# A residual stack of four attention and feed-forward pairs: the first attention in units of 512 tokens, and all attentions with token-major values

## The reference

```python
x = x + xattn0(layernorm(x), ctx, mask, Wq, Wkv, Wo)             # a0: 2 heads of 64, full mask
x = x + ffn0(layernorm(x), w_gate, w_up, w_down)                 # f0: quantised gated FFN
x = x + xattn1(layernorm(x), ctx, ...)                           # a1: 16 heads of 8, biases
x = x + ffn1(layernorm(x), expert_sel, keys, values, ...)        # f1: 16 small experts, top 4
x = x + xattn2(layernorm(x), ctx, mask, ...)                     # a2: 16 heads of 8, rotary, key mask
x = x + ffn2(layernorm(x), ...)                                  # f2: product keys, gated FFN
x = x + xattn3(layernorm(x), ctx, ...)                           # a3: 16 heads of 8, biases
x = x + ffn3(layernorm(x), ...)                                  # f3: 8 experts, top 2, shared ones

def attention(x, context):                                       # the core of a0 to a3
    q, k, v = split_heads(x @ Wq + bq), split_heads(context @ Wk + bk), split_heads(context @ Wv + bv)
    scores = einsum('bhqd,bhkd->bhqk', q, k) * scale             # masked with -inf in a0 and a2
    out = einsum('bhqk,bhkd->bhqd', softmax(scores), v)
    return merge_heads(out) @ Wo + bo
```

## Time and profile before

| | |
|---|---|
| median of the runs | 1361.57 us |
| profiled execution, its own time | 1361.15 us |
| its span, first to last instruction | 1359.4 us |
| mean granted TensorE clock | 0.901 |
| busy: TensorE, VectorE, ScalarE, GpSimd | 1061.9, 988.6, 624.9, 339.9 us |
| a0, first matmul to f0's layer norm | 16.93 to 141.43 us |
| f0 to the first step of a1's layer norm | to 307.32 us |
| steady batches of a1 | 6.07 us apart |
| steady batches of a2 | 6.92 us apart |

### The profile page before, as it was taken

The page is one execution under the profiler, slowest core; times in us unless marked ns, Lnnn a source line. Parts: engine busy times, 40 slices in busy tenths (PEclk is TensorE's granted clock), DMA queues, the critical chain, the costliest instruction groups (busy, mean ns, idle before and its releaser), DMA issues.

```text
span 1359.4 us, 21524 instructions
## 1 busy us (share of the span) xinstructions
PE 1061.9 (78%) x7235; PEld 685.3 (50%) x7235; DVE 988.6 (73%) x2359; ACT 624.9 (46%) x972; POOL 339.9 (25%) x350
## 2 busy tenths in 40 slices
PE   2766780067996998799669888888878969999998
PEld 1544430064553775454326666566654536566665
DVE  4687669977786566577689788788567875666665
ACT  2211356735763334665266555555447633333332
POOL 0121000001220001444198767677201210000000
PEclk9888796578998999899859888888999998999999
DMA  7000000001000000000000000000000000000000
GB/s 264 0 1 0 0 0 0 0 1 58 2 2 1 1 1 0 1 2 1 1 1 1 2 1 0 1 0 0 1 1 2 1 1 1 16 8 8 8 8 16
DMA packets 7797, 14.12 MB, mean 10 GB/s; under 512 B 800, under 2 KB 5024, under 8 KB 7328
## 3 DMA queue, kind: packets, MB, share of 16 engines
q1 hardware_dynamic: 7712, 13.05, 2.9%
HBM read 10.95 MB, written 2.10 MB: 10 GB/s over the span
## 4 chain that ended last, share of the span: by engine, by line
PE 44%; DVE 37%; issue 11%; ACT 6%; DVEq 1%; SPq 1%; DMA 0%; POOL 0%; ACTq 0%
DVE big L1127 6%; DVE big L1122 6%; PE psum L1997 4%; PE psum L919 4%; PE psum L2000 4%; PE psum L2011 4%; PE psum L1692 3%; DVE big L1903 2%; PE psum L1484 2%; DVE tmp L1868 2%; PE psum L1437 2%; PE psum L1446 2%; PE psum L247 2%; ACT psum L1760 2%; DVE amax L1247 2%
## 5 line engine op out<-in xcount | busy, mean ns | idle before, releaser
L1122 DVE TENSOR_REDUCE big<-psum 128x16 f32<-128x1024 f32 x96 | 114.4, 1221 | 74.7 <-PE psum L873 38.7
L1817 POOL TENSOR_TENSOR big<-big 128x512 f32<-128x512 f32 x128 | 134.7, 1087 | 20.7 <-ACT big L1740 20.7
L2047 ACT ACTIVATE big<-psum 128x512 f32<-128x512 f32 x80 | 47.9, 598 | 143.3 <-PE psum L1997 143.2
L1760 ACT ACTIVATE psum<-big,tmp 128x512 f32<-128x512 f32 x128 | 85.0, 687 | 42.3 <-DVE big L1903 38.4
L1903 DVE SCALAR_TENSOR_TENSOR big<-big,tmp,psum 128x512 f32<-128x512 f32 x128 | 90.4, 743 | 4.7 <-ACT psum L1760 1.8
L790 POOL TENSOR_TENSOR big<-big,w_const 128x256 f32<-128x256 f32 x48 | 34.8, 726 | 233.3 <-PE psum L919 219.3
L2100 DVE TENSOR_TENSOR big<-big,psum 128x512 f32<-128x512 f32 x80 | 54.4, 687 | 53.1 <-PE psum L2000 52.5
L1827 POOL TENSOR_TENSOR big<-big 128x1024 f32<-128x1024 f32 x32 | 75.4, 2367 | 70.4 <-DVE big L1903 70.4
L1127 DVE RECIPROCAL big<-psum 128x256 f32<-128x256 f32 x48 | 84.0, 1749 | 11.8 <-PE psum L919 11.8
L2011 PEld LDWEIGHTS psum<-tmp,big 128*128 128x128 f32 x512 | 66.7, 191 | 40.1 <-issue 36.4
L1028 ACT ACTIVATE big<-psum 128x1024 f32<-128x1024 f32 x64 | 62.0, 1021 | 51.5 <-PE psum L903 51.5
(11 more groups left out here) (252 smaller groups left out, 2484.2 us busy)
## 6 DMA issues: line engine op xcount, KB each, us to landing
out<-X SPq DMA_DIRECT2D x8, 256.0 KB, 2.3
tmp<-in_pack_f SPq DMA_DIRECT2D x1, 1924.0 KB, 7.5
w_f<-in_pack_f SPq DMA_DIRECT2D x1, 1280.0 KB, 12.3
ctxd<-in_ctxd SPq DMA_DIRECT2D x1, 1024.0 KB, 6.4
tmp<-in_pack_once SPq DMA_DIRECT2D x1, 960.0 KB, 8.6
w_a<-in_pack_a SPq DMA_DIRECT2D x3, 256.0 KB, 12.0
w_f<-in_pack_f SPq DMA_DIRECT2D x1, 576.0 KB, 9.5
w_const<-in_pack_const SPq DMA_DIRECT2D x1, 560.0 KB, 3.9
```

What stands on the lines that cost most here:

```text
L1122: dve.tensor_reduce(nm, psum[:, 1 + 2 * t:3 + 2 * t, :].rearrange("p c (r l k) -> p (c r) l k", r=2, k=SK), AX.X, ALU.max, negate=True).th ...
L1760: act.activation(bank(EX_BANK + h % 2), ssum[t][:, h * 512:(h + 1) * 512], ACT.Exp, bias=shift2[:, t * NH2 + h:t * NH2 + h + 1]).then_inc( ...
L1817: ins = pool.tensor_tensor(ssum[t][:, h * 512:(h + 1) * 512].rearrange("p (i j) -> p i j", i=ROWS2), st[:, 0, h, 0:ROWS2].unsqueeze(2).to_ ...
```

## The change

**a0** is a new function set (`att0_pe`, `att0_act`, `att0_dve`, `att0_pool`), unrolled over eight units of 512 tokens. Keys and values of all batches are built once, by ScalarE with a mask as its scale. The negated maxima are no longer transposed: GpSimd adds them to the mask (`less_max`), and the matmul with the identity in ST that brought the mask now brings both. PV has the probabilities as its stationary operand and, as moving one, two heads' values of 64 columns, each with a column of ones behind it (130 columns). Its output is token-major, with one sum per head and token, so that the reciprocal has 8 elements; `TO` transposes the result for `O`. From group 3 on GpSimd normalises. The three steps on f0's quantised weights stand in units 3 to 5, with the rounding made by an int16 output.

**a1 to a3** get the same PV: probabilities stationary (128x128), two heads' values of 8 columns and a ones column each moving (18). The sums are 32 per token, `norm` writes `ow`, `TO` transposes it, `take_out` on ScalarE evicts, and `O` follows one iteration later. In the iteration PV's second half, MX and Q now stand ahead of O, NM, TO. GpSimd no longer builds values.

**The layer norm** has 10 VectorE steps with fewer waits, and takes 1/sqrt as exp(-0.5 ln) in two ScalarE steps from one table set; in a0 it is done in two parts (12 and 20 tiles). **The context** is loaded once (512 KB); a value block is two matmuls with 64 output partitions each. X is loaded in two parts, and the first 12 tiles stand ahead of everything.

```diff
@@ loads
-            sp.dma_start(pack_sb["const"][:, :], dram["pack_const"]).then_inc(S("ld_const"), 16)
-            sp.dma_start(X[:, :, :], dram["x"].rearrange("(t p) d -> p t d", p=P)).then_inc(S("ld_x"), 16)
+            sp.dma_start(X[:, 0:LN0, :], x_in[:, 0:LN0, :]).then_inc(S("ld_x"), 16)
+            sp.dma_start(pack_sb["const"][:, :], dram["pack_const"]).then_inc(S("ld_const"), 16)
             sp.dma_start(pack_sb["a0"][:, :], dram["pack_a0"]).then_inc(S("ld_a0"), 16)
-            sp.dma_start(ctxd[:, :, :, :].rearrange("p b a k -> p (b a k)"), dram["ctxd"]).then_inc(S("ld_ctx"), 16)
+            sp.dma_start(ctx_sb[:, :, :].rearrange("p b k -> p (b k)"), dram["ctx"]).then_inc(S("ld_ctx"), 16)
             sp.dma_start(mask_u8[:, :], dram["mask"]).then_inc(S("ld_mask"), 16)
+            sp.dma_start(X[:, LN0:N_TILES, :], x_in[:, LN0:N_TILES, :]).then_inc(S("ld_x"), 16)
@@ heads_pe
-            def PV(b, which):
+            def PV(b, t):
...
-                for e in range(2):
-                    for r in range(4):
-                        w = W["vmask8"][:, 32 * e:32 * e + 32] if which else \
-                            L.vw[b % 2][:, 64 * r + 32 * e:64 * r + 32 * e + 32]
-                        ins = pe.matmul(bank(6)[32 * r:32 * r + 32, 256 * which:256 * which + 256], w,
-                                        L.pt[b % 2][:, (2 * r + e) * 256:(2 * r + e + 1) * 256],
-                                        start=(e == 0), stop=(e == 1))
+                for c in range(8):
+                    ins = pe.matmul(bank(6)[:, 144 * t + 18 * c:144 * t + 18 * c + 18],
+                                    L.pt[b % 2][:, c * 256 + t * P:c * 256 + (t + 1) * P],
+                                    L.vw[:, b, c].rearrange("p e n -> p (e n)"), start=True, stop=True)
+            def TO(b):
+                pe.wait_ge(hs("ow"), hat(s, "ow") + b + 1)
+                pe.wait_ge(hs("nmT"), hat(s, "nmT") + min(b + 4, B))
...
+                for t in range(2):
+                    ins = pe.transpose(bank(5)[:, 256 + t * P:256 + (t + 1) * P], L.ow[b % 2][:, t * P:(t + 1) * P], ident)
@@ heads_act
                 exp(b, 1)
                 if b + 1 < B:
                     takeN(b + 1)
+                if b >= 2:
+                    take_out(b - 2)
                 norm_half(b)
@@ heads_dve
-                dve.reciprocal(L.rz, bank(6)[:, 256:512]).then_inc(hs("rz"), 1)
+                both = bank(6)[:, 0:288].rearrange("p (h n) -> p h n", n=9)
+                dve.reciprocal(L.rz[b % 2], both[:, :, 8]).then_inc(hs("rz"), 1)
...
-                dve.tensor_tensor(L.oT[b % 2], bank(6)[:, 0:256], L.rz, ALU.mult).then_inc(hs("oT"), 1)
+                dve.tensor_tensor(L.ow[b % 2].rearrange("p (h n) -> p h n", n=8), both[:, :, 0:8],
+                                  L.rz[b % 2].unsqueeze(2).to_broadcast([P, 32, 8]), ALU.mult).then_inc(hs("ow"), 1)
@@ att0_pe, the loop
+            for i in range(N_GROUPS):
+                ST(i)
+                if i + 2 < N_GROUPS:
+                    Q(i + 2)
+                if i + 1 < N_GROUPS:
+                    MX(i + 1)
+                PV(i)
+                if i:
+                    O(i - 1)
+                if i + 3 < N_GROUPS:
+                    T(i + 3)
+                TO(i)
@@ att0_dve, ahead of and in the loop
+            mx(1)
+            dve.wait_ge(S("bn0"), N_TILES)
+            dve.sem_inc(sem(s, "stats"), 1)
+            ln_finish_dve(dve, s, 1)
+            for i in range(N_GROUPS):
+                if i and i + 1 < N_GROUPS:
+                    mx(i + 1)
+                over(i)
+                if i:
+                    add(i - 1)
+                    tail_stats(dve, s, i - 1, False)
+                if 3 <= i < 6:
+                    f0_weights_dve(dve, i - 3)
@@ att0_pool
+            for g in range(N_GROUPS):
+                less_max(g)
+                if g + 3 < N_GROUPS:
+                    norm(g + 3)
@@ ln_finish_act
-            act.activation(lnw[:, 5, :], lnw[:, 4, :], ACT.Sqrt).then_inc(sem(s, "std"), 1)
+            act.activation(lnw[:, 5, lo:hi], lnw[:, 4, lo:hi], ACT.Ln).then_inc(S("all_lnv"), 1)
+            act.wait_ge(S("all_lnv"), SUB.index(s) + k + (s != "a0") + 1)
+            act.activation(lnw[:, 6, lo:hi], lnw[:, 5, lo:hi], ACT.Exp, scale=-0.5).then_inc(sem(s, "std"), 1)
```

More of the change, by code:

```diff
@@ L722, in build, with ctx_keys, context_values @@
-        HSUB = ("a1", "a2", "a3")
-        PER = dict(k_ps=1, v_ps=4, k=8, kb=2, ka=2, v=4, zero=2, mask=0, kv=B, q_ps=B, qe=0, qT=B, q16=B, mx_ps=2 * B,
-                   mx=2 * B, nm_ps=B, nmT=B, st_ps=B, pt=2 * B, pv=B, rz=B, oT=B, o_ps=B, r=0, prep=0)
-        PRIMED = dict(mx=2, nmT=1, pt=2, pv=4, oT=1, o_ps=2)
+        ctx_sb = sb("ctx", [P, B, SK])
+        def ctx_keys(b, n):
+            return ctx_sb[:, b:b + n, :]
+        def context_values(pe, out, b, w):
+            for a in range(2):
+                ins = pe.matmul(out[64 * a:64 * a + 64, :], ctx_sb[:, b, :], w, start=True, stop=True)
+            return ins
@@ L746, in __init__ @@
                 self.kbd16 = a.take(B * 512, BF16).rearrange("p (b u n) -> p b u n", b=B, u=2)
-                self.V2 = a.take(B * P).rearrange("p (b n) -> p b n", b=B)
-                self.vw = [a.take(256) for _ in range(2)]
+                self.vw = a.take(B * 144).rearrange("p (b c e n) -> p b c e n", b=B, c=8, e=2)
                 self.pt = [a.take(2048) for _ in range(2)]
@@ L754, in __init__ @@
                 self.oT = [a.take(256) for _ in range(2)]
-                self.rz = a.take(256)
+                self.ow = [a.take(256) for _ in range(2)]
+                self.rz = [a.take(32) for _ in range(2)]
                 if rope:
@@ L807, in heads_pool @@
                 rotate(1)
-                weights(0)
                 rotate(2)
-                weights(1)
                 rotate(3)
@@ L840, in V @@
                 if i:
[L841 removed]
+                    pe.wait_ge(hs("v"), hat(s, "v") + 2 * i)
                 for m in range(4):
[L843 to L844 removed]
+                    ins = context_values(pe, bank(5)[:, m * P:(m + 1) * P], 4 * i + m, W[s + "_wv"])
                 ins.then_inc(hs("v_ps"), 1)
@@ L960, in heads_pe @@
                 turn_ahead(b)
-            for b in range(B + 2):
+            for b in range(B + 4):
                 if b < B:
@@ L1073, in heads_act @@
                 act.wait_ge(hs("mask"), hat(s, "mask") + 2)
-            for b in range(B):
+            for b in range(B + 2):
+                if b >= B:
+                    take_out(b - 2)
+                    continue
                 exp(b, 0)
@@ new lines, in build @@
+        m16 = a0m.take(N_TILES * P, BF16).rearrange("p (t n) -> p t n", t=N_TILES)
+        mm16 = [a0m.take(GN, BF16) for _ in range(2)]
+        pt0 = [a0m.take(GN) for _ in range(2)]
+        qT0 = [a0m.take(GN) for _ in range(3)]
+        q16_0 = [a0m.take(GN, BF16) for _ in range(2)]
+        nm0 = [a0m.take(8) for _ in range(2)]
+        rz0 = [a0m.take(8) for _ in range(2)]
+        ow0 = [a0m.take(GN) for _ in range(2)]
+        oT0 = [a0m.take(GN) for _ in range(2)]
+        wlev = [a0m.take(I0, I16) for _ in range(3)]
```

819 lines of the change are left out of this document (331 added, 488 removed).

## The result

The changed kernel takes 1643.96 us (median of 4 runs, 1634.65 to 1652.26) against 1361.24 us for the kernel before, measured beside it: a ratio of 1.2078 with a 95% interval of 1.2003 to 1.2153. The forecast was 1397 us, in a range of 1355 to 1435. The direction was right and the size was not: 247 us are missing.

What follows compares the result with a forecast made beforehand. The first attention had slack on every engine; in sixteen-head attentions TensorE was nearly full, with VectorE's reciprocal in the ring. Profiled 1361.15 - 63 (first attention) - 4 (layer norm) + 103 (sixteen-head attentions) = 1397 us, range 1355 to 1435.

Steps and rivals of the forecast that it cites:

- work of the new list: TensorE in a1 to a3: added work of 1.1 us per batch (1.3 in a2), 62 us with the prologues.
- waits of the order: Batches of a1 to a3: two waits for ScalarE, 1.0 of the 2.1 us added per batch; +41 in all.
- rival 3: a1 to a3: 18-column streams drop TensorE's clock to 1.2 GHz; over 1450, up to 1540 us; chance 0.08.
- PV's list: TensorE, a1 to a3: 32 records per batch at 0.101 us, 3.24 us in place of 2.00; bounds 2.00 and 4.2.
- The list of 7.15 us: TensorE's work per batch in a1: 5.63 - 2.00 + 3.24 + 0.28 us, above the old period by 1.1.
- Rival 1: a1 to a3: loading probabilities costs no more than the old PV, 2.0 us; total 1344 us; chance 0.08.
- The hand-overs: a1 to a3: TensorE waits twice per batch for ScalarE, about 1.0 of the 2.1 us added.
- rival 2: a1 to a3: waits for ScalarE cost nothing, only work counts, +62; total 1356 us; chance 0.12.
- the count: One batch of a1 timed from NM's start to the next NM: period 8.2 us, 2.1 over the old one.
- was to end at 78: First attention: 26 us until the first ST, then TensorE-led groups of 5.5; 78 against 141.4 us, -63.
- rival 4: First attention bound by its chain, not TensorE's list: 7.5 to 8 us per group; total 1415 us; chance 0.15.
- 0.5 us in seven places: Layer norms: two steps go, one ScalarE step comes, some waits go; -4 us, bounds 0 and -8.

Runs made afterwards that it cites:

- old heads: The changed kernel with the code of before for a1, a2 and a3, single context kept; a0, layer norms and loads stay changed: 1286.82 us.
- 128 columns, early order: The changed kernel with PV moving 128 columns, NM behind the first MX, take_out behind the reads of Q: 1355.37 us; its chain of waits is TensorE alone.
- early order: The changed kernel with NM behind the first MX on TensorE and take_out behind the reads of Q on ScalarE; with 18 columns kept: 1434.38 us.
- 128 columns, its order: The changed kernel, order untouched, with each PV matmul in a1 to a3 moving 128 columns in place of 18: 1447.93 us.

## Why the prediction was wrong, by its own steps

The sum over a1, a2 and a3, counted against the old heads beside the new a0 (122.4, 140.7, 120.3 us):

| | forecast, against before | measured |
|---|---|---|
| work of the new list | +62 | +68 (128 columns, early order, less old heads) |
| waits of the order | +41 | +89 (128 columns: its order less early order, with the clock that they cost) |
| clock | 0 | +190 (after less 128 columns, its order) |
| sum | +103 | +347 |

The split is along one path from one kernel to the next. In the early order the narrow streams cost 77 us (20.7 + 9.4 + 46.5; the last is the one long spell in a3), in the order of the change 190: waits and narrow streams make each other dearer, and the clock's share here holds both.

- **The clock is the step that failed.** It was rival 3, with a chance of 0.08 and "over 1450, up to 1540". I held against it that TensorE would be busy 85% of the time. The rows show that this is no argument: TensorE was busy all the time both in 78 us at 1.00 and in 78 us at 0.50, and in the changed kernel it was busy 25.48 of 26 us at 0.50. What the forecast put at nothing cost 190 us of the 347. Even the rival's price was too low, since I doubled only the records with long streams. PV's short ones double as well, 1.89 to 3.53 us per 16.
- **PV's list** came from the router at 0.101 per record: 3.24 us per batch. Measured are 0.118 (1.89 / 16) at full clock with 18 columns and 0.124 (1.98 / 16) with 128, so 3.8 to 4.0 us, inside its bounds. The mean of the router's eight records was misleading: the second starts 0.03 us after the first, the others 0.112 apart, and 0.112 is also the distance within PV. The list of 7.15 us became 7.37 and 7.81 with 128 columns, mean 7.6: 0.45 us too little.
- **Rival 1** (loads cost nothing) was to hold under 0.07 us per record and is refuted by the same numbers. The Trainium skill ("Perfetto Trace Analysis", Identifying the Most-Contended Engine) judges room on TensorE by the share of weight loads, beside the share of its peak work. In the kernel whose chain is all TensorE that share is 103.74 of 144 us, 72%, with no room at all, so the trace doesn't agree.
- **The hand-overs** through takeN, TO and take_out are there, which refutes rival 2: 0.52 us ahead of TO in a1, where the count had 0.72. Missing was T's wait for the normalised half and the reads of Q behind take_out, 1.95 us in every second batch of a1, and the clock that falls behind it. With 128 columns the maxima of a1 start 8.1 and 12.3 us apart in turn, mean 10.2; the count had 8.2. The waits cost 28 to 32 us per attention at 128 columns, where the forecast had 41 for all three.
- **a0** was to end at 78 and ended at 84.2. The sum left out GpSimd's conversion of the mask, eight times 1.9 us or more ahead of less_max(0). Without it a0 ends at 79.0, near the forecast, but by luck: the first ST then starts at 22.3 us and not at 26, and from there to the end it takes 56.7 us and not 52. (With the mask on GpSimd the first ST starts at 26.9.) GpSimd's normalisation costs 0.79 us per tile, above both estimates (0.27 and 0.55). The units come 5.2 to 6.2 us apart once the first two are through, which refutes rival 4 (1415) with its 7.5.
- **The layer norm** was to give 0.5 us in seven places. f0's goes from 3.07 us to 2.2, and each of the seven is 0.8 to 0.9 us shorter. The f-stages together are 10.6 us shorter, 7.4 of it in f2 alone, where only 0.85 lie in the layer norm. The rest of f2's gain shows in every kernel run here that has the change. The instructions of f2 are the same, and the gain comes in a few steps between 90 and 190 us of the stage; its cause stays open.

Had the clock held, the time would have been near 1361 - 57 (a0) - 11 (the f-stages) - 6 (a1 to a3 with the old heads beside the new a0) + 157 (work and waits) = 1444 us. The 128-column kernel in the same order took 1447.93. This is bookkeeping and no second proof, since the 157 come from that kernel. So the order of causes is: the clock, then the waits, then the work.

## What to carry to other kernels

Moving the large operand from the streaming to the stationary side turns long streams into loads with almost nothing to stream: price such a record from a long run of its kind, and reckon with the clock even where TensorE's list is full: it can be lost without a gap, and above all it comes back late. Moving columns that nobody needs can be the cheapest cure, since a record costs its load anyway: 18 to 128 columns took 196 us off this kernel. Before relieving one engine by loading another, ask for the plain alternative; here bfloat16 in the old layout did all that it did in the new one.

## What the hardware showed that I had not expected

- A float32 record with a load of 128 columns takes 0.118 us with 18 moving columns and 0.124 us with 128, at full clock: the stream is all but free. From start to start it is 0.112 us with 16, 18, 64 and 128 columns alike; only the first record of a run differs (0.13 us with 18, 0.21 with 128). At 1.2 GHz it is 0.213.
- In bfloat16 the same record with 18 columns starts 0.025 us after the one before, less than a quarter of float32, and not half.
- The same list in the same order had a mean clock of 0.96 or more with 128 or 64 moving columns and of 0.70 (a3), 0.81 (a1) and 0.90 (a2) with 18. These are means of full clock and 1.2 GHz: with 18 columns TensorE ran the full list at either for 78 us without a gap. With bfloat16 and 18 columns it was 0.91 without the order's waits and 0.70 with them.
- a3 fell more than a1 with the same instructions (0.70 and 0.81), by one long spell at 1.2 GHz in the one trace of this kernel. Why it came there is open.
- GpSimd took 16.43 us for eight conversions of 128x512 from uint8, about 2 us each; VectorE made the same mask in two instructions in 2.36 us, in time that it had idle ahead of its first maximum.
